# Attention's output bias in a two-layer kernel: written to PSUM by ScalarE, in place of a TensorE product of ones by bias

## What is computed

```python
x = x + _layernorm(attn(_layernorm(x)))      # first attention
x = x + _layernorm(ffn(_layernorm(x)))       # gated linear attention, 4 experts, top 1

# attn, the part the change touches
q, k = relu(q), relu(k)
ksum = k.sum(axis=-1)
z = 1.0 / (einsum('bhd,bhdn->bhn', ksum, q) + eps)
context = einsum('bhdn,bhen->bhde', v, k)
out = einsum('bhde,bhen->bhdn', context, q) * z
return out @ w_proj.T + b_proj               # <- this bias
```

## Time and profile before

| | us |
|---|---|
| median of 3 runs | 2476.82 (2476.65 to 2481.74) |
| the profiled execution's own time | 2477.75 |
| its span | 2475.9 |
| busy in the span: TensorE | 2413.4 (97%) |
| VectorE | 1807.0 (73%) |
| ScalarE | 1577.3 (64%) |
| GpSimd | 1137.2 (46%) |

### The profile page before, as it was taken

The page is one execution under the profiler, slowest core; times in us unless marked ns, Lnnn a source line. Parts: engine busy times, 40 slices in busy tenths (PEclk is TensorE's granted clock), DMA queues, the critical chain, the costliest instruction groups (busy, mean ns, idle before and its releaser), DMA issues.

```text
span 2475.9 us, 56923 instructions
## 1 busy us (share of the span) xinstructions
PE 2413.4 (97%) x20208; PEld 1426.7 (58%) x20208; DVE 1807.0 (73%) x3548; ACT 1577.3 (64%) x3473; POOL 1137.2 (46%) x929
## 2 busy tenths in 40 slices
PE   5999999998999999999999999999999999999997
PEld 2444444454666666666666666666666666666664
DVE  5444444426888888888888888888888888888885
ACT  3222322226777777777777777777777777777774
POOL 2587533314444444444444444444444444444444
PEclk9999999999999999999999999999999999999999
DMA  5634433311111111111111111111111111111111
GB/s 137 204 101 123 103 101 101 84 54 39 44 51 42 47 42 42 42 42 42 47 47 50 43 47 43 43 42 42 42 47 47 50 44 47 42 42 42 42 27 34
DMA packets 250704, 145.65 MB, mean 59 GB/s; under 512 B 208096, under 2 KB 208096, under 8 KB 250144
## 3 DMA queue, kind: packets, MB, share of 16 engines
q1 hardware_dynamic: 240048, 119.32, 19.5%
q10 hardware_dynamic: 9504, 17.31, 1.9%
q0 software_dynamic: 1104, 8.40, 0.9%
HBM read 61.09 MB, written 33.55 MB: 38 GB/s over the span
## 4 chain that ended last, share of the span: by engine, by line
PE 75%; ACT 10%; issue 6%; DVE 5%; POOL 3%; DMA 1%; ACTq 0%; POOLq 0%; SPq 0%; DVEq 0%
PE psum L319 15%; PE psum L320 14%; PE psum L321 14%; PE psum L592 6%; PE psum L457 5%; PE psum L494 5%; PE psum L474 3%; PE psum L503 3%; PE psum L514 2%; PE psum L331 2%; DVE region L1376 2%; DVE region L1190 2%; ACT region L722 2%; ACT junk L684 2%; ACT region L792 1%
## 5 line engine op out<-in xcount | busy, mean ns | idle before, releaser
L319 PE MATMUL psum<-wb,region 128*128 128x512 f16 x768 | 292.9, 381 | 0.0
L320 PE MATMUL psum<-wb,region 128*128 128x512 f16 x768 | 291.6, 380 | 0.0
L321 PE MATMUL psum<-wb,region 128*128 128x512 f16 x768 | 291.4, 379 | 0.0
L1077 POOL TENSOR_TENSOR region<-region,kfac 128x512 f32<-128x512 f32 x64 | 66.7, 1042 | 474.4 <-DVE kfac L1335 474.4
L1060 POOL TENSOR_TENSOR region<-region 128x1024 f32<-128x1024 f32 x64 | 147.8, 2309 | 259.5 <-DVE region L1443 231.0
L1443 DVE SCALAR_TENSOR_TENSOR region<-psum,region 128x512 f16<-128x512 f32 x64 | 44.3, 692 | 223.2 <-ACT region L887 223.2
L1065 POOL TENSOR_TENSOR region<-region 128x1024 f32<-128x1024 f32 x64 | 150.7, 2354 | 93.3 <-DVE region L1208 93.3
L1072 POOL TENSOR_SCALAR region<-region,m 128x512 f32<-128x512 f32 x256 | 172.3, 692 | 25.7 <-DVE hm L1279 25.7
L592 PE MATMUL psum<-region 128*128 128x512 f16 x768 | 176.2, 379 | 2.1 <-DVE region L1443 2.1
L1081 POOL TENSOR_TENSOR region<-region 128x512 f32<-128x512 f32 x64 | 81.8, 1278 | 202.6 <-ACT region L795 202.6
L1242 DVE SCALAR_TENSOR_TENSOR region<-psum,m,region 128x512 f32<-128x512 f32 x192 | 144.2, 751 | 6.8
(11 more groups left out here) (236 smaller groups left out, 7238.9 us busy)
## 6 DMA issues: line engine op xcount, KB each, us to landing
region<-x_in SPq DMA_DIRECT2D x128, 256.0 KB, 2.6
q_cols<-region ACTq DMA_DIRECT2D x64, 256.0 KB, 2.5
region<-q_cols SPq DMA_DIRECT2D x64, 256.0 KB, 2.8
out_rows<-region SPq DMA_DIRECT2D x62, 256.0 KB, 2.0
region<-wb_in POOLq DMA_DIRECT2D x1, 3072.0 KB, 13.3
region<-wqkv_in SPq DMA_DIRECT2D x4, 512.0 KB, 6.3
region<-region SPq DMA_TRANSPOSE x128, 3.0
region<-ws_in POOLq DMA_DIRECT2D x1, 1280.0 KB, 7.5
```

Source lines behind the costliest of these rows:

```text
L319: mm(out, lhs(0), rhs(0), start=start, stop=False)
L320: mm(out, lhs(0), rhs(1), start=False, stop=False)
L321: return mm(out, lhs(1), rhs(0), start=False, stop=stop)
```

## The change

Four edits:

1. `y_mm` has no product of ones by bias any more. A new ScalarE step, `ahead_bias`, copies `bproj` times 64 to bank 0 once `qzf_ok` says that VectorE has read `z` there, and signals `bias_ok`; `y_mm` waits for that too, and all twelve products add to what is in the bank. `ahead_bias` stands behind `ahead_z`, ahead of `front_exps`.
2. So that the products add to it, only the first of `den`'s four products has the flag that starts a sum.
3. `scores` waits for one semaphore a path in place of two: the first copy of each pair signals nothing, the second `path1_ok` or `path2_ok`.
4. `bias16` and its two GpSimd instructions go.

```diff
             def den(n, p, b, at=0, back=True):
-                    last = mm(bank[at][:, g * P:(g + 1) * P], kden[:, b, g, :], qb[:, p, g, :], start=True, stop=True)
+                    last = mm(bank[at][:, g * P:(g + 1) * P], kden[:, b, g, :], qb[:, p, g, :],
+                              start=(g == 0), stop=True, skip_group_check=True)
             def y_mm(n, b, at=0):
                 pe.wait_ge(S("qz_ok"), cur(n))
-                mm(bank[at], ones16[:, :], bias16[:, :], start=True, stop=False)
+                pe.wait_ge(S("bias_ok"), n + 1)
                 for g in range(KT):
-                    last = mm3(bank[at], lambda x: qz16[:, x, g, :], lambda x: mix[b][:, x, g, :], False, g == KT - 1)
+                    mm(bank[at], qz16[:, 0, g, :], mix[b][:, 0, g, :], start=False, stop=False, skip_group_check=True)
+                    mm(bank[at], qz16[:, 0, g, :], mix[b][:, 1, g, :], start=False, stop=False, skip_group_check=True)
+                    last = mm(bank[at], qz16[:, 1, g, :], mix[b][:, 0, g, :], start=False, stop=(g == KT - 1), skip_group_check=True)
             def scores(n, path):
-                pe.wait_ge(S(q_ready), cur(n))
-                pe.wait_ge(S(k_ready), cur(n))
+                pe.wait_ge(S(ready), cur(n))
             def inter_sparse(n, front):
-                pe.wait_ge(S("q2T_ok"), cur(n))
+                pe.wait_ge(S("path2_ok"), cur(n))
+            def ahead_bias(n, at=0):
+                act.wait_ge(S("qzf_ok"), n + 1)
+                ac(bank[at], bproj[:, :], ACT.Copy, scale=QZ_SCALE).then_inc(S("bias_ok"), 1)
             def front_transposed(n):
-                to_cols(n, q1T, 5, 0, "q1T_ok")
-                to_cols(n, k1T, 2, 1, "k1T_ok")
+                to_cols(n, q1T, 5, 0)
+                to_cols(n, k1T, 2, 1).then_inc(S("path1_ok"), 1)
             def front_transposed2(n):
-                to_cols(n, q2T, 4, 2, "q2T_ok")
-                to_cols(n, k2T, 6, 3, "k2T_ok")
+                to_cols(n, q2T, 4, 2)
+                to_cols(n, k2T, 6, 3).then_inc(S("path2_ok"), 1)
             # ScalarE's step
                 if ahead:
                     ahead_z(n + 2)
+                    ahead_bias(n + 2)
                 if front:
                     front_exps(n)
             # ScalarE, ahead of the steps
             ahead_z(1, at=5)
+            ahead_bias(0)
             ahead_norm1(0)
+            ahead_bias(1, at=5)
             def late_bias():
-                then_step(nc.gpsimd.tensor_scalar(bias16[:, :], bproj[:, :], 1.0, 1.0, ALU.mult, ALU.mult))
-                low = slice(HALF, P)
-                then_step(nc.gpsimd.tensor_tensor(bias16[low, :], bproj[low, :], bias16[low, :], ALU.subtract))
```

More of the change, by code:

```diff
@@ L82, in sandwich_kernel @@
         mix = [sb("mix0", 2, KT, C, dt=f16), sb("mix1", 2, KT, C, dt=f16)]
-        bias16 = sb("bias16", C, dt=f16)
         rk, ksum_q = sb("rk", BATCH, KT), sb("ksum_q", BATCH, KT)
@@ L191, in sandwich_kernel @@
                        "low1_ok", "labi_ok", "lexp_ok", "abs_ok", "ex_ok", "ln_ok", "sig_ok",
-                       "v_ok", "ke_ok", "e1_ok", "e2_ok", "exs_ok", "q1T_ok", "k1T_ok", "q2T_ok", "k2T_ok",
+                       "v_ok", "ke_ok", "e1_ok", "e2_ok", "exs_ok", "path1_ok", "path2_ok",
                        "osq_ok", "z_ok", "ogh_ok", "xc_ok", "xnh_ok", "x1m_ok"],
@@ L450, in scores @@
             def scores(n, path):
-                kT, qT, where, k_ready, q_ready = ((k1T, q1T, (2, 5), "k1T_ok", "q1T_ok"), (k2T, q2T, (4, 6), "k2T_ok", "q2T_ok"))[path]
-                pe.wait_ge(S(q_ready), cur(n))
-                pe.wait_ge(S(k_ready), cur(n))
+                kT, qT, where, ready = ((k1T, q1T, (2, 5), "path1_ok"), (k2T, q2T, (4, 6), "path2_ok"))[path]
+                pe.wait_ge(S(ready), cur(n))
                 for pr in range(PAIRS):
@@ L688, in rstd_of, with to_cols @@
                 ac(rstd[:, k, :], lnv[:, k, :], ACT.Exp, scale=-0.5).then_inc(S(f"rstd{k}"), 1)
-            def to_cols(n, dst, where, k, done):
+            def to_cols(n, dst, where, k):
                 act.wait_ge(S("tr_pe"), n * 4 + 2 + k)
-                ac(dst.rearrange("p a b -> p (a b)"), bank[where], ACT.Copy).then_inc(S(done), 1)
+                return ac(dst.rearrange("p a b -> p (a b)"), bank[where], ACT.Copy)
             def front_mean(n, p):
```

## The result

| | before | after |
|---|---|---|
| median, us | 2477.48 (4 runs) | 2491.66 (4 runs, 2490.39 to 2493.12) |
| ratio, 95% interval | | 1.0053 [1.0037, 1.0069] |
| the profiled execution's own time | 2477.75 | 2490.39 |
| its span | 2475.9 | 2488.6 |

The change makes the kernel slower by half a per cent: 14.2 us of median, where the forecast had 16.4 us (2493.2 us). Run once more, on another chip, it came out at 1.0049 [1.0036, 1.0063].

What follows compares the result with a forecast made beforehand. The ScalarE and VectorE stretch from cum1_pe to x1_ok was taken as the bound: 32 x 0.23 + 28 x 0.33 = 16.6 us, less 0.2, on 2476.8 gives 2493.2 us. Range 2484 to 2507 us, forecast chance 0.80.

Steps and rivals of the forecast that it cites:

- What bounds the kernel: From cum1_pe to x1_ok, about 7.4 us a step, ScalarE and VectorE set the time; TensorE waits at L474.
- The product that goes: TensorE's bias product L336, 0.22 us a tile, 13.8 us in all: worth nothing, L474's wait grows to 0.81 us.
- The copy that comes: ScalarE's new bias copy, judged by L702: holds ScalarE up 0.54 us, low end 0.48, high end 0.77.
- Where it lands: Copy starts 0.04 us after the last L1359; exponentials 0.23 us later, 0.33 in 28 steps opening a loop iteration.
- What the delay reaches: Whole delay arrives at x1_ok and in the period; TensorE's wait about 1.04 us; VectorE's and GpSimd's slack holds.
- the prediction's first rival: TensorE's own work sets the time once its L474 wait of 0.51 to 0.59 us is gone; chance 0.05.
- The rest: Merged semaphores, flag and GpSimd instructions: nothing; steps 0 and 1 and the start: together -0.2 us.
- the 6.5 us at the low end of the range: Merged waits in scores: 128 queue instructions of 51 ns, 6.5 us if each held TensorE up; taken as nothing.
- a loss of 0.2 us: Ahead of step 0 the first copy stands behind L728: sum 0.45 us later, less 0.22 for the product.
- TensorE sets the time: Rival: TensorE doesn't wait for the stretch cum1_pe to x1_ok, so 13.8 us come off, 2463.0 us; chance 0.05.
- The copy hides: Rival: slack behind VectorE swallows the 0.23 us, only the start counts, 2476.6 us, up to 2481; chance 0.08.
- The copy costs more: Rival: ScalarE holds the exponentials until the copy's write completes, 0.5 us more a step, 2523 us; chance 0.07.

Runs made afterwards that it cites:

- e1: Kernel before without the product of ones by bias and nothing in its place (bias left out); 2477.90 us, ratio 0.9991.
- e3: Kernel after with ScalarE's copy of the bias made twice, the second waiting for the first; 2528.96 us, ratio 1.0194.
- e6: Kernel before with ScalarE's two back_rms instructions moved from ahead of the tail's deviation to behind front_exs, nothing left out; 2462.12 us, ratio 0.9940.
- e2: Kernel before with only the semaphores of each path in scores merged; 2478.17 us, ratio 0.9994.
- e9: Kernel after with back_rms and front_residual moved behind ahead_norm1 on ScalarE, nothing left out; 2446.93 us, ratio 0.9878.
- e4: Kernel after with only the first 128 of 512 columns of the bias copied; 2475.13 us, ratio 0.9985.
- e5: Kernel after with z written to SBUF instead of bank 0, so the whole copy runs in ScalarE's idle time; 2477.12 us, ratio 0.9997.
- e10: Kernel after with back_rms and front_residual behind ahead_norm1 on ScalarE and z in SBUF; 2453.06 us, ratio 0.9899.

## Why the prediction was right

**What bounds the kernel.** Right. The stretch from `cum1_pe` to `x1_ok` sets the period: e1 (less TensorE work, same period), e3 (0.64 us in, 0.62 out) and e6 (shorter stretch, shorter period) show it from three sides.

**The product that goes.** Worth nothing in the steps: shown by e1. The wait grew by its 0.217 us.

**The copy that comes.** Right within 0.03 us. Its length is 0.60 us and it holds ScalarE for 0.53 us; taken from L702 were 0.63 and 0.54.

**Where it lands.** 0.04 us behind the last L1364, as put. The period grew by 0.21 and 0.30 to 0.31 us, against 0.23 and 0.33: between the step 2 and step 61 exponentials 15.2 us more, against 16.3 for 59 periods.

**What the delay reaches.** All of it, to the period. VectorE's and GpSimd's slack held. TensorE's wait was given as 1.04 us and is 1.01 to 1.04 on the weight loads; on the products it is 0.36 + 0.22 + 0.21 = 0.79 us. The prediction took TensorE's idle time from the row of the weight loads, and it is smaller. For this change that made no difference, since a delay adds to the wait whatever its size. For a shortened stretch it did: the point from which TensorE's own work sets the time, which the prediction's first rival puts at 0.51 to 0.59 us less, lies at 0.28 to 0.36 us less, as e6 showed.

**The rest.** The merged semaphores: nothing, shown by e2; the 6.5 us at the low end of the range weren't needed. The start and the end are where the sum was off. To the exponentials of step 2 the kernel after was 1.1 us ahead, that is 1.5 without step 2's own delay, against 0.2 forecast. Of these, 0.9 us are there when `x1` of the first tile is done (555.48 against 556.37 us), where the prediction had put a loss of 0.2 us; e2, which up to there is the kernel before, is ahead by 1.0 us at the same point. The later start of the first sum isn't on the path there, since `x1` (L1190) comes straight behind a memset on VectorE, here in the kernel before:

```profile
554.67 0.91 DVE L1512 MEMSET region<- 128x1024 f32 x1 [0.16 <-issue]
555.62 0.75 DVE L1190 SCALAR_TENSOR_TENSOR region<-psum,rstd,region 128x512 f32<-128x512 f32 x1
```

In the kernel after the memset ends at 554.70 us and `x1` starts at 554.73. So that loss of 0.2 us was put on a wrong path. From the last `x1` to the end the kernel after took 83.90 us against 85.19, at a granted clock of 0.95 against 0.93:

```profile
2404.70:2488.60 83.90, 66.37 (x642) 41.08 (x642) 52.89 (x102) 41.04 (x91) 37.11 (x32) 0.95 0.13 29
```

60 delays of 15.5 us in all, less 1.5, less 1.3: 12.7 us of span, where 16.4 stood. The kernel after run again had 84.6 us for the end, so these two terms move at least in part with the execution, and that the profiled pair came out 3.7 us below the forecast is in part chance.

**The rivals.** TensorE sets the time: fell with e1; the 97% that spoke for it is the time in which products were in flight, while the weight loads were busy for 58%. It is true in e9, where the stretch is shorter. The copy hides: fell with the period. The copy costs more: fell, the exponential follows after 0.53 us.

## What to carry to other kernels

The engine with the highest busy share need not be the one whose work is on the path: follow the chain through one period, see where it leaves that engine, and price work of that engine between that point and its return at nothing, and any work added to the detour in full. That holds while the engine stands still at the return, here for 0.28 to 0.36 us a step; with the detour shorter by that much, its own work counts again. Cover has to be measured from the moment at which the new work may start, not by the idle time in front of the next instruction: of 1.50 us idle the copy could use 0.2 to 0.3. And a change that loses can be the right one behind another: with the detour shortened first, the same edit is worth what it was meant to be, 0.22 us a step.

## What the runs showed of the hardware that was not expected

- The idle time of weight loads overstates a stall of TensorE: 0.59 us there was 0.36 us of the products (1.90 against 2.26 us for 16 of them), 1.02 us was 0.79, and 0.17 us in e6 was none. The difference is 0.23 to 0.24 us in the kernels before and after and in e1, e3, e4 and e5.
- A VectorE instruction with both tensors in SBUF ended 0.15 us after the GpSimd instruction that was running, 0.40 or 0.50 us long in place of 0.35. The same instruction with one of the two in PSUM kept its 0.35 us beside the same GpSimd product, which in the kernel before runs until 1526.24 + 1.04 = 1527.28 us, while VectorE starts at 1526.92. The row of the GpSimd product:

```profile
1526.24 1.04 POOL L1077 TENSOR_TENSOR region<-region,kfac 128x512 f32<-128x512 f32 x1 [7.51 <-DVE kfac L1335]
```

The Trainium skill (GPSIMD Engine Reference, section 1. Specifications) names this contention, for VectorE instructions with two SBUF inputs. e10's trace agrees, with its 0.15 us in all 60 steps. ScalarE's copy (L736) stands beside it too, but the second of the four VectorE instructions, from 1543.17 us on, runs beside that copy without the GpSimd product and takes 0.34 us; so does the first instruction of tiles 0 and 1, 0.35 and 0.34 us, with neither beside it. So the GpSimd product is what the longer ones have in common; that it is the contention of that page and not another effect of the product was not tried by itself.
